# Scores of two heads as two 64-row tiles of TensorE, with the queries stacked two heads to 128 partitions

## Chip, core and metric

The kernel runs on one core of a Trainium2 chip. The metric is the device time of one execution in microseconds (us), the median over several runs.

## What is computed

The input x has 8 batches of 256 tokens with 256 features. It is normalised to xn, and two branches are computed from xn and joined:

```python
xn = _layernorm(x, axis=-1)
s  = attention_1(xn)       # 16 heads, head size 80 (64 rotary + 16), low-rank weights, causal softmax
h  = attention_2(xn)       # inside _L0_ffn_ref: RMS norm, 16 heads of size 16, causal softmax
g  = _silu(xn + h @ Wo.T + moe(rmsnorm(xn + h @ Wo.T)))   # 8 experts, top 2
out = x + s * g
```

The change touches attention_2 (called "mha" in the kernel) alone: `attn = softmax(causal(q @ k.T / 4))` for 16 heads of size 16 and 256 tokens, and `attn @ v`.

## The kernel before, in words

The work runs over eight batches b; batches 1 to 6 are a hardware loop, 0 and 7 are written out. After them come 23 expert blocks (the last 300 us), which the change doesn't touch. Each batch has four stages, and each engine runs its own list in this order; semaphores alone tie the engines together.

- **P2** (`stage_p2`, L689): TensorE turns the stacked queries and keys of attention_2 (`qs`, `ks`, one token to a partition) by eight steps u of four 128x128 transposes each. Steps with even u are queries, with odd u keys; `bank2(u)` (L356) rotates over three PSUM banks, so step u waits until bank u-3 has been copied out. A transposed bank holds four head pairs: the even head of a pair on partitions 0 to 63, the odd one on 64 to 127. The keys are kept like that (`kt2`, two heads to 128 partitions). The queries are not: `qt2` has a slot of 128 partitions for each of the 16 heads, the other half of which is zero (set once by POOL, L485), so that a matmul over all 128 rows against the pair's keys gives one head's scores. ACT copies the even heads (L1073, semaphore `t2e`) and DVE the odd heads (`odd_heads`, L1422, semaphore `t2o`). DVE also normalises the previous batch's attention_2 here (L1307).
- **T1** (`stage_t1`, L779): for every head h of attention_1, `scores1` (L769) computes its transposed scores into bank 4 + h % 2, ACT takes the exponential (L1094) and DVE masks it (`causal`, L1386). Between them stand the plain scores of attention_2 for the row maximum: `max2` (L727) computes head h into bank 2 + h % 2, and DVE takes its maximum in two instructions (`maxima`, L1399 and L1402). TensorE's order in `heads` (L757) is: scores of head h, then the maximum's scores of head h-1, then for h = 7, 11, 15 the products with the values of four heads (`values`, L744), then what `after` hangs on head h: the previous batch's transposes back (0) and output projection (3), the transposes of the next x (10), the router's transposes (11, they wait for DVE's L1496) and logits (14). DVE's order (`stage_m2`, L1388) is: causal(h), maxima(h), then what hangs on h: the residual (4), statistics (5), a copy of x (7), the scaling for the router (9, L1496), the low part of x (12). After head 15 DVE picks the top two experts (L1507 to L1522), and TensorE waits for that early in P1.
- **P1** (`stage_p1`, L638): the projections of the next batch, transposed head by head.
- **T2** (`stage_t2`, L786): for every head h of attention_2, `scores2` (L773) computes its transposed scores (two matmuls with the queries and keys, two that add the mask from bf16 tiles) into bank 4 + h % 2 for ACT's exponential. Between them stand the plain scores of attention_1 of the next batch, `max1` (L714), with DVE's maxima. ACT also rounds keys for max1 (`rounded`, L1019) after every even head from 2 to 12, DVE rounds queries (L1358).

The rule that one bank belongs to even heads and the other to odd heads holds in both stages: head h waits only for the release of head h-2 (`mx2`, `mx1`, `ex1`, `ex2`, each to the count h-1).

Of the kernel before, what the change touches and what calls it, by code (L numbers as in the profile page):

```python
# [91 lines left out]
def build(nc, x, w_cols, w_dq, w_uqr, w_dkv, w_ukv, w_out, w_o, w_ln1, w_ln2, w_r, w_experts,  # L92
          cosines, sines, ident, mask, mask_t, seen_t, upper, route_c, slots, out):
    ctx = ExitStack()
    with ctx:
# [84 lines left out]
        qt2 = sb("qt2", [P, H, S], F32R, late)  # L180
# [100 lines left out]
        t2o = sem("mha_q_odd_kept")  # L281
# [187 lines left out]
        def _(pool):  # L469
# [14 lines left out]
            nc.gpsimd.memset(ks[:, :, :, MROW2:MROW2 + 1].bitcast(F32), 1.0)  # L484
            nc.gpsimd.memset(qt2[:, :, :].bitcast(F32), 0.0).then_inc(clear, 1)  # L485
# [87 lines left out]
        def _(pe):  # L573
# [195 lines left out]
            def scores1(h, o):  # L769
                mm(o[:, P:2 * P], kt[:, h, P:S], qt[:, h, P:S], True, True)  # L770
                return mm(o[:, 2 * P:4 * P], kt[:, h, 0:P], qt[:, h, :], True, True)

            def scores2(h, o):  # L773
                mm(o[:, 0:2 * P], kt2[:, h // 2, P:S], qt2[:, h, :], True, False)
                mm(o[:, 2 * P:4 * P], kt2[:, h // 2, 0:P], qt2[:, h, :], False, False)
                mm(o[:, P:2 * P], idb[:, :], maskb[:, :], False, True)
                return mm(o[:, 2 * P:3 * P], idb[:, :], maskb[:, :], False, True)

            def stage_t1(b, after):  # L779
# [4 lines left out]
                return heads(b, scores1, st1, ex1, exm1, pv1, ov1, v1, before_h0, lambda: wait(pe, x2d, b), max2(b), after)  # L784
# [978 lines left out]
```

## Time and profile before

| | us |
|---|---|
| median of 3 runs | 976.75 |
| lowest, highest | 970.0, 980.24 |
| the profiled execution | 980.88 |
| its span, first to last instruction | 979.1 |
| TensorE busy in the span | 838.6 (86%) |
| DVE busy | 662.8 (68%) |
| ACT busy | 502.0 (51%) |
| granted TensorE clock, mean | 0.945 |

The time of an execution is 1.8 us above its span. A batch of the loop takes 78.5 us (TensorE's transposes of the row maxima start at 300.95 and again at 379.49). Busy times are shares of the whole span and mix the stages; the stages have different limits, so the rows below are taken from one batch, the one between these two times.

### The profile page before, as it was taken

How to read it: one execution, taken by the hardware profiler on the slowest of the kernel's cores; microseconds unless marked ns; L12 is line 12 of the kernel's file. 1: busy time of each engine (PE TensorE's matmuls, PEld its weight loads, DVE VectorE, ACT ScalarE, POOL GpSimd, SP SyncE). 2: the span in 40 equal slices, each digit the busy share in tenths (PEclk: the TensorE clock that was granted, in tenths of full speed). 3: DMA queues.
4: the chain of work that ended last, by engine and by line, in shares of the span. 5: the costliest groups of instructions: out<-in, count | busy, mean ns of one | idle time of the engine just before them, and what ended most of it. 6: DMA issues, size and time to landing. Idle time of an engine off the chain costs nothing.

```text
span 979.1 us, 20037 instructions
## 1 busy us (share of the span) xinstructions
PE 838.6 (86%) x6688; PEld 748.5 (76%) x6688; DVE 662.8 (68%) x2345; ACT 502.0 (51%) x1090; POOL 268.6 (27%) x286
## 2 busy tenths in 40 slices
PE   5879999999989999998998999976169999999940
PEld 3858988977887887797797797764169999999940
DVE  4877668667667766857866866833257777777726
ACT  3436465365356456355445536533046777777721
POOL 5520400320230221131041032010404454545333
PEclk9988999999999999999999999977589999999985
DMA  8000000000000000000000000030245656588434
GB/s 272 1 1 2 13 2 12 13 2 2 22 0 2 12 11 2 12 11 2 11 12 1 12 12 1 2 141 22 41 137 188 241 191 240 191 302 302 166 119 171
DMA packets 33535, 70.88 MB, mean 72 GB/s; under 512 B 10786, under 2 KB 24994, under 8 KB 30498
## 3 DMA queue, kind: packets, MB, share of 16 engines
q1 hardware_dynamic: 26866, 57.39, 16.8%
q0 software_dynamic: 5440, 12.13, 4.0%
q10 hardware_dynamic: 1152, 0.49, 0.3%
q8 instruction: 29, 0.48, 0.2%
q14 instruction: 48, 0.39, 0.2%
HBM read 57.35 MB, written 12.71 MB: 72 GB/s over the span
## 4 chain that ended last, share of the span: by engine, by line
PE 67%; DVE 14%; issue 9%; DMA 3%; SPq 3%; ACT 2%; POOL 1%; DVEq 0%; ACTq 0%; POOLq 0%
PE ps L575 55%; PE ps L668 5%; PE ps L705 3%; DVE ps L1399 2%; DVE ps L1402 2%; DVE negm L1402 1%; PE ps L601 1%; SPq L422 1%; DMA ln<-in_w_ln 1%; DVE negm L1399 1%; PE ps L902 1%; DMA yl<-expert_rows 1%; PE ps L610 1%; SPq L437 1%; DMA raw<-in_w_experts 1%
## 5 line engine op out<-in xcount | busy, mean ns | idle before, releaser
L1094 ACT ACTIVATE ex<-ps 128x384 f32<-128x384 f32 x256 | 125.6, 496 | 137.9 <-PE ps L575 126.6
L575 PE MATMUL ps<-qt,kt 128*128 128x256 f32 (+1 forms) x768 | 164.9, 325 | 9.5 <-issue 6.0
L503 POOL TENSOR_TENSOR tok<-tok,swp 128x256 f32<-128x256 f32 x128 | 97.2, 760 | 219.2 <-DVE swp L1354 218.2
L1399 DVE CUSTOM_DVE_ANT_0 ps<-ps,mask 128x128 f32<-128x128 f32 x256 | 76.4, 298 | 77.7 <-PE ps L575 45.3
L575 PEld LDWEIGHTS ps<-qt,kt 128*128 128x128 f32 x768 | 109.2, 193 | 18.6 <-issue 10.4
L1402 DVE CUSTOM_DVE_ANT_0 ps<-ps,mask 128x256 f32<-128x256 f32 x256 | 119.3, 466 | 0.0
L1233 DVE TENSOR_TENSOR wel<-raw,weh 128x768 fp32r<-128x768 f32 x92 | 88.2, 958 | 37.8 <-ACT weh L962 36.4
L575 PE MATMUL ps<-wh,xth 128*128 128x320 f32 (+2 forms) x352 | 95.7, 354 | 6.3 <-DVE wl L1233 3.7
L1350 DVE TENSOR_TENSOR tok<-ps,cos_t 128x320 f32<-128x320 f32 x128 | 62.8, 491 | 52.6 <-PE ps L575 46.8
L546 POOL DMA_INDIRECT expert_rows<-yo,slot_of x46 | 57.5, 1249 | 128.9 <-ACT yo L1195 121.9
L575 PE MATMUL ps<-xeh,weh 128*128 128x256 f32 x368 | 78.5, 295 | 11.7 <-issue 11.7
L962 ACT ACTIVATE qt<-ps 128x512 f32<-128x512 f32 (+1 forms) x96 | 57.1, 594 | 61.4 <-PE ps L668 54.7
L962 ACT ACTIVATE kt<-ps 128x512 f32<-128x512 f32 (+1 forms) x96 | 57.3, 597 | 57.4 <-PE ps L668 49.4
L962 ACT ACTIVATE weh<-raw 128x768 fp32r<-128x768 f32 x92 | 77.8, 846 | 9.9 <-DMA raw<-in_w_experts 9.7
L575 PE MATMUL ps<-wl,xth 128*128 128x320 f32 (+2 forms) x352 | 82.5, 316 | 0.0
L575 PE MATMUL ps<-wh,xtl 128*128 128x320 f32 (+2 forms) x352 | 82.4, 316 | 0.0
L668 PE MATMUL ps<-idf,tok 128*128 128x128 f32 x512 | 76.8, 272 | 0.0
L575 PE MATMUL ps<-kr,qr 128*128 128x128 f32 (+1 forms) x256 | 61.5, 325 | 17.0 <-DVE negm L1402 13.6
L575 PE MATMUL ps<-kt,qt 128*128 128x128 f32 (+1 forms) x256 | 72.0, 363 | 4.1 <-DVE negm L1402 4.1
L575 PE MATMUL ps<-xeh,wel 128*128 128x256 f32 x368 | 74.8, 285 | 0.0
L575 PE MATMUL ps<-xel,weh 128*128 128x256 f32 x368 | 74.8, 285 | 0.0
L575 PEld LDWEIGHTS ps<-xeh,weh 128*128 128x128 f32 x368 | 57.9, 195 | 15.7 <-issue 15.7
(167 smaller groups left out, 1958.4 us busy)
## 6 DMA issues: line engine op xcount, KB each, us to landing
raw<-in_w_experts SPq DMA_DIRECT2D x23, 1536.0 KB
yl<-expert_rows SPq DMA_DIRECT2D x4, 1024.0 KB, 5.4
mla_branch<-s_b SPq DMA_DIRECT2D x8, 256.0 KB, 2.1
x_normalised<-otk SPq DMA_DIRECT2D x8, 256.0 KB, 2.2
xr<-in_x SPq DMA_DIRECT2D x1, 2048.0 KB
s_tok<-mla_branch SPq DMA_DIRECT2D x1, 2048.0 KB
out<-xr SPq DMA_DIRECT2D x4, 512.0 KB, 2.9
w_cols_raw<-in_w_cols SPq DMA_DIRECT2D x1, 1792.0 KB, 15.9
```

The source lines that it names most:

```text
L422: sp.dma_start(mt_b[:, blk, :, :], rows.rearrange("(j p) f -> p j f", p=P)).then_inc(mtd[blk], 16)
L503: nc.gpsimd.tensor_tensor(t, t, swp[:, n % 2, :, :], ALU.add).then_inc(tokd, 1)
L546: nc.gpsimd.indirect_dma_start(ys[:, :], bass.IndirectOffsetOnAxis(mt_b[:, blk, j, 1:2], 0), yo[:, blk % 2, j, :], None).then_inc(ysd[blk ...
L575: return nc.tensor.matmul(o, a, m, start=start, stop=stop, skip_group_check=True, **k)
L668: t = nc.tensor.transpose(ps[2 + n % 2][:, j * P:(j + 1) * P], tok[:, n % 4, j, :], idf[:, :])
L705: i = nc.tensor.transpose(bank2(u)[:, j * P:(j + 1) * P], a[:, p0:p0 + P], idf[:, :])
L962: return nc.scalar.activation(o, a, ACT.Copy)
L1094: nc.scalar.activation(ex[:, h % (2 * G), :], ps[4 + h % 2][:, P:4 * P], ACT.Exp, scale=scale).then_inc(ex_, 1)
L1233: return nc.vector.tensor_tensor(o, a, b.bitcast(F32), ALU.subtract)
L1350: nc.vector.tensor_tensor(tok[:, n % 4, :, 0:HW], a, cos_t[:, tt:tt + 1, :].broadcast_to([P, G, HW]), ALU.mult)
L1399: nc.vector.tensor_tensor_reduce(out=o[:, 0:P], in0=o[:, 0:P], in1=mask2[:, 1, :], scale=-1.0, scalar=-2.0 * BIG, op0=ALU.add, op1=ALU.min ...
L1402: nc.vector.tensor_tensor_reduce(out=o[:, S:2 * S], in0=o[:, S:2 * S], in1=mask2[:, :, :].rearrange("p a k -> p (a k)"), scale=-1.0, scala ...
```

## The change

`qt2` becomes as wide as `kt2`: two heads to 128 partitions, no zero halves. POOL's memset of `qt2`, DVE's four `odd_heads` copies and the semaphore `t2o` go; ACT copies each transposed query bank whole. The scores are computed per pair of heads, on odd h in `max2` and on even h in `scores2`, with `tile_position=(0, 0)` for the even head and `(64, 0)` for the odd head of the pair, each into its own bank. Both banks must be free before the pair starts. The order of the pair's matmuls alternates between the tiles; the mask is added by 128-row matmuls as before.

```diff
-        qt2 = sb("qt2", [P, H, S], F32R, late)
+        qt2 = sb("qt2", [P, H // 2, S], F32R, late)
...
-            nc.gpsimd.memset(qt2[:, :, :].bitcast(F32), 0.0).then_inc(clear, 1)
...
                     if u >= 3:
 
                         wait(pe, t2e, 8 * b + u - 2)
-                        if (u - 3) % 2 == 0:
-                            wait(pe, t2o, 4 * b + (u - 3) // 2 + 1)
...
             def max2(b):
                 def head(h):
-                    if h == 0:
+                    if h % 2 == 0:
+                        return
+                    if h == 1:
                         wait(pe, t2e, 8 * b + 8)
-                        wait(pe, t2o, 4 * b + 4)
-                    if h >= 2:
+                    else:
                         wait(pe, mx2, 16 * b + h - 1)
-                    raw_scores(ps[2 + h % 2], qt2[:, h, :], kt2[:, h // 2, :]).then_inc(m2d, 1)
+                    for q0, k1, o0, first in ((0, P, 0, True), (P, S, S, False)):
+                        for e in range(2):
+                            r = slice(ST * e, ST * (e + 1))
+                            i = mm(ps[2 + e][:, o0:o0 + k1], qt2[r, h // 2, q0:q0 + P], kt2[r, h // 2, 0:k1],
+                                   first, True, tile_position=(ST * e, 0))
+                            if not first:
+                                i.then_inc(m2d, 1)
...
-            def scores2(h, o):
-                mm(o[:, 0:2 * P], kt2[:, h // 2, P:S], qt2[:, h, :], True, False)
-                mm(o[:, 2 * P:4 * P], kt2[:, h // 2, 0:P], qt2[:, h, :], False, False)
-                mm(o[:, P:2 * P], idb[:, :], maskb[:, :], False, True)
-                return mm(o[:, 2 * P:3 * P], idb[:, :], maskb[:, :], False, True)
+            def scores2(b):
+                def head(h):
+                    if h % 2:
+                        return
+                    if h >= 2:
+                        wait(pe, ex2, 16 * b + h)
+                    for k in range(1, -1, -1):
+                        for e in range(2):
+                            r = slice(ST * e, ST * (e + 1))
+                            mm(ps[4 + e][:, (1 - k) * S:(2 - k) * S], kt2[r, h // 2, k * P:(k + 1) * P],
+                               qt2[r, h // 2, :], k == 1, False, tile_position=(ST * e, 0))
+                    for e in range(2):
+                        mm(ps[4 + e][:, P:2 * P], idb[:, :], maskb[:, :], False, True)
+                        mm(ps[4 + e][:, 2 * P:3 * P], idb[:, :], maskb[:, :], False, True).then_inc(st2, 1)
+                return head
...
-                    if u % 2 == 0:
-
-                        h0 = 8 * (u // 2 % 2)
-                        copy(qt2[0:ST, h0:h0 + 8:2, t], a[0:ST, :, :]).then_inc(t2e, 1)
-                    else:
-                        copy(kt2[:, 4 * (u // 2 % 2):4 * (u // 2 % 2) + 4, t], a).then_inc(t2e, 1)
+                    h0 = 4 * (u // 2 % 2)
+                    copy((qt2, kt2)[u % 2][:, h0:h0 + 4, t], a).then_inc(t2e, 1)
...
-                wait(dve, st2, 16 * b)
-                odd_heads(b, 0)
-                odd_heads(b, 1)
-                odd_heads(b, 2)
                 normalise()
-                odd_heads(b, 3)
```

`scores1` keeps its instructions and its wait for head h-2; only its place in the code moves. The two small DMAs that write the maxima into row 48 and 112 of `qt2` (L393) write whole rows instead of every second head's.

## Rows read from the trace of the kernel before

**Rows 1.** The page: the chain that ended last, by engine, then by line.
```profile
PE 67%; DVE 14%; issue 9%; DMA 3%; SPq 3%; ACT 2%; POOL 1%; DVEq 0%; ACTq 0%; POOLq 0%
PE ps L575 55%; PE ps L668 5%; PE ps L705 3%; DVE ps L1399 2%; DVE ps L1402 2%; DVE negm L1402 1%; PE ps L601 1%; SPq L422 1%; DMA ln<-in_w_ln 1%; DVE negm L1399 1%; PE ps L902 1%; DMA yl<-expert_rows 1%; PE ps L610 1%; SPq L437 1%; DMA raw<-in_w_experts 1%
```

**Rows 2.** Windows T1, P1, T2, P2: length, PE, PEld, DVE, ACT, POOL busy; PEclk; DMA.
```profile
307.60:331.50 23.90, 22.56 (x190) 18.47 (x188) 20.04 (x103) 11.06 (x26) 0.86 (x1) 1.00 0.03 11
331.50:357.60 26.10, 26.10 (x192) 25.45 (x193) 15.56 (x39) 11.05 (x21) 11.93 (x16) 1.00 0.03 11
357.60:379.50 21.90, 18.72 (x187) 14.79 (x186) 16.50 (x92) 13.09 (x32) 3.92 (x4) 1.00 0.01 1
300.95:307.60 6.65, 6.28 (x52) 5.58 (x53) 3.78 (x8) 5.00 (x11) 0.00 (x0) 1.00 0.02 5
```

**Rows 3.** Tile qt (qt and qt2 together): copies and memset, min/median/max ns, first and last start.
```profile
L1229 DVE CAST qt<-ps x32: 686/695/696, 75.2 to 620.5; 64x512 fp32r<-64x512 f32 x32
L485 POOL MEMSET qt<- x1: 3517/3517/3517, 7.6 to 7.6; 128x4096 f32 x1
```

**Rows 4.** Timeline of P2, PE then ACT: start us, us, operation, [idle before <-releaser].
```profile
303.90 0.66 PE L705 MATMUL ps<-idf,ks 128*128 128x128 f32 x4 [0.37 <-DVE qt L1229]
...
307.14 0.49 ACT L1094 ACTIVATE ex<-ps 128x384 f32<-128x384 f32 x1
```

**Rows 5.** Timeline of T1, PE. qt,kt: scores1; kt,qt: max2; wo,otf: project; ex,v: values.
```profile
310.11 1.89 PE L575 MATMUL ps<-wo,otf 128*128 128x256 f32 x8
311.84 0.82 PE L575 MATMUL ps<-qt,kt 128*128 128x128 f32 x4
312.31 0.58 PE L575 MATMUL ps<-kt,qt 128*128 128x128 f32 x2
312.72 0.82 PE L575 MATMUL ps<-qt,kt 128*128 128x128 f32 x4
...
315.46 0.86 PE L575 MATMUL ps<-ex,v 128*32 128x256 f32 x16
316.25 0.92 PE L575 MATMUL ps<-qt,kt 128*128 128x128 f32 x4
316.82 0.58 PE L575 MATMUL ps<-kt,qt 128*128 128x128 f32 x2
```

**Rows 6.** Timeline of T1, DVE: maxima of head 3, causal of head 4.
```profile
313.03 0.30 DVE L1399 CUSTOM_DVE_ANT_0 ps<-ps,mask 128x128 f32<-128x128 f32 x1 [1.50 <-PE ps L575]
...
313.63 0.14 DVE L1402 DVE_READ_ACCUMULATOR2_ANT negm<- 128x1 f32 x1
313.63 0.42 DVE L1386 TENSOR_TENSOR ex<-ex,seen 128x256 f32<-128x256 f32 x1
313.96 0.29 DVE L1399 CUSTOM_DVE_ANT_0 ps<-ps,mask 128x128 f32<-128x128 f32 x1
```

**Rows 7.** Waits of DVE inside T1: us in total, times, longest us.
```profile
DVE ps L1399 <- PE ps L575: 3.3, 5, 1.5
```

**Rows 8.** Timeline of T2, PE: scores2, its mask, max1.
```profile
365.10 0.40 PE L575 MATMUL ps<-qt,kt 128*128 128x256 f32 x2
365.34 0.29 PE L575 MATMUL ps<-maskb,idb 128*128 128x128 bf16 x2
365.43 0.48 PE L575 MATMUL ps<-kr,qr 128*128 128x128 f32 x2
```

**Rows 9.** Timeline of T2, ACT and DVE around a joint wait.
```profile
365.66 0.49 ACT L1094 ACTIVATE ex<-ps 128x384 f32<-128x384 f32 x1 [3.04 <-PE ps L575]
366.05 0.62 ACT L962 ACTIVATE kr<-kt 128x512 fp32r<-128x512 f32 x1
366.56 0.48 ACT L1094 ACTIVATE ex<-ps 128x384 f32<-128x384 f32 x1
369.38 0.49 ACT L1094 ACTIVATE ex<-ps 128x384 f32<-128x384 f32 x1 [2.33 <-PE ps L575]
369.53 0.30 DVE L1399 CUSTOM_DVE_ANT_0 ps<-ps,mask 128x128 f32<-128x128 f32 x1 [1.42 <-PE ps L575]
```

More of the change, by code:

```diff
@@ L483, in _ @@
             nc.gpsimd.memset(tok[:, 1:4:2, :, MROW:MROW + 1], 1.0)
-            nc.gpsimd.memset(ks[:, :, :, MROW2:MROW2 + 1].bitcast(F32), 1.0)
-            nc.gpsimd.memset(qt2[:, :, :].bitcast(F32), 0.0).then_inc(clear, 1)
+            nc.gpsimd.memset(ks[:, :, :, MROW2:MROW2 + 1].bitcast(F32), 1.0).then_inc(clear, 1)
             def power(k, t):
@@ L757, in heads @@
                 for h in range(H):
-                    if h >= 2:
-                        wait(pe, ex_, 16 * b + h - 1)
-                    scores_t(h, ps[4 + h % 2]).then_inc(st, 1)
+                    scores_t(h)
                     if h > 0:
@@ L767, in heads, with scores1, head @@
                 return lambda: values(NG - 1)
-            def scores1(h, o):
-                mm(o[:, P:2 * P], kt[:, h, P:S], qt[:, h, P:S], True, True)
-                return mm(o[:, 2 * P:4 * P], kt[:, h, 0:P], qt[:, h, :], True, True)
-            def scores2(h, o):
-                mm(o[:, 0:2 * P], kt2[:, h // 2, P:S], qt2[:, h, :], True, False)
-                mm(o[:, 2 * P:4 * P], kt2[:, h // 2, 0:P], qt2[:, h, :], False, False)
-                mm(o[:, P:2 * P], idb[:, :], maskb[:, :], False, True)
-                return mm(o[:, 2 * P:3 * P], idb[:, :], maskb[:, :], False, True)
+            def scores1(b):
+                def head(h):
+                    o = ps[4 + h % 2]
+                    if h >= 2:
+                        wait(pe, ex1, 16 * b + h - 1)
+                    mm(o[:, P:2 * P], kt[:, h, P:S], qt[:, h, P:S], True, True)
+                    mm(o[:, 2 * P:4 * P], kt[:, h, 0:P], qt[:, h, :], True, True).then_inc(st1, 1)
+                return head
+            def scores2(b):
+                def head(h):
+                    if h % 2:
+                        return
+                    if h >= 2:
+                        wait(pe, ex2, 16 * b + h)
[7 more added lines that the diff above has]
+                        mm(ps[4 + e][:, 2 * P:3 * P], idb[:, :], maskb[:, :], False, True).then_inc(st2, 1)
+                return head
             def stage_t1(b, after):
@@ L783, in before_h0 @@
                     wait(pe, v1d, 2 * b + 2)
-                return heads(b, scores1, st1, ex1, exm1, pv1, ov1, v1, before_h0, lambda: wait(pe, x2d, b), max2(b), after)
+                return heads(b, scores1(b), exm1, pv1, ov1, v1, before_h0, lambda: wait(pe, x2d, b), max2(b), after)
             def stage_t2(b, max_head, after):
@@ L790, in before_h0 @@
                     wait(pe, v2d, b + 1)
-                heads(b, scores2, st2, ex2, ex2, pv2, ov2, v2, before_h0, lambda: wait(pe, sd, b + 1), max_head,
+                heads(b, scores2(b), ex2, pv2, ov2, v2, before_h0, lambda: wait(pe, sd, b + 1), max_head,
                       after)()
@@ L1420, in low2 @@
                     op0=ALU.mult, op1=ALU.subtract).then_inc(s2d, 1)
-            def odd_heads(b, i):
-                wait(dve, tr2, 8 * b + 2 * i + 1)
-                t = slice(i // 2 * P, (i // 2 + 1) * P)
-                h0 = 8 * (i % 2)
-                copy(qt2[ST:P, h0 + 1:h0 + 8:2, t],
-                     bank2(2 * i)[ST:P, :].rearrange("p (h t) -> p h t", h=4)).then_inc(t2o, 1)
             def batch(b, first, more):
                 normalise, kept = ((lambda: None),) * 2 if first else close2(b - 1)
-                wait(dve, st2, 16 * b)
-                odd_heads(b, 0)
-                odd_heads(b, 1)
-                odd_heads(b, 2)
                 normalise()
-                odd_heads(b, 3)
                 after = {4: kept}
```

5 lines of the change are left out of this document (2 added, 3 removed).

## Prediction

> **What bounds the kernel now.** First the chain that ended last [rows 1]: 67% of it is TensorE, 55% in the one matmul helper, 14% DVE, and nearly all of DVE's named lines are the row maxima (L1399, L1402). So TensorE leads, and DVE leads in places. Where, the windows of one batch tell [rows 2]. P1 (26.1 us) is TensorE without a gap, and the change doesn't touch it. T1 is 23.9 us with TensorE busy 22.6 and DVE 20.0: two engines close to full, coupled head by head. T2 is 21.9 us with 18.7, 16.5 and 13.1 (ACT): nobody is full, so what counts there is the hand-over between them. P2 is 6.65 us. The granted clock is 1.00, that is 2.4 GHz, in all four. The change takes work off TensorE and DVE in T1, T2 and P2 and pays in hand-overs, so I walk the stages with the durations of single instructions rather than with busy shares. Waits of DVE for the max scores in T1 are only 3.3 us in five places [rows 7]: that is all that faster matmuls could give back to DVE there.
>
> **Small parts.** POOL's memset ran from 7.6 to 11.1 us [rows 3] while the first weights were still on their way; POOL's next work depends on DVE's statistics of x, so it gives 0. If that cover were gone it would be at most its 3.5 us, once. DVE's 32 copies of 0.69 us [rows 3] go: 2.8 us of DVE per batch, all in P2. ACT's query copy becomes 128 partitions in place of 64; its 64-partition form takes about what the neighbouring full copies do (0.6 us either way in P2), so I add 0. The DMAs into the mask rows keep their bytes; 0.
>
> **P2: -0.5 us per batch.** Transposing step u = 3 started at 303.90 after an idle 0.37 whose releaser is DVE's copy [rows 4]. Without that copy, steps are limited by TensorE (0.44 us a step) and ACT (0.5 us a copy): ACT's eighth copy ends, and the exponential of head 0 starts, near 306.65 in place of 307.14 [rows 4], and TensorE's first scores move from 306.28 to about 305.7. Bounds 0 to -0.9; I take -0.5. DVE's normalising moves earlier too, but its user was not late.
>
> **T1: what a pair costs.** Today head h's max scores go into one bank while DVE reads the other. DVE takes 0.60 us for a maximum (313.03 to 313.63) and 0.33 for the mask of a head (313.63 to 313.96) [rows 6], 0.93 together; TensorE takes 0.47 for scores1 and 0.41 for max2, 0.88 together [rows 5]. They run side by side with a bank in hand. After the change one pair fills both banks, so TensorE may start it only when DVE has read both. That is a ping-pong:
> - end of DVE's last maximum to the pair's start: the accumulator read ends 0.14 after DVE could go on [rows 6], plus 0.05 for the semaphore (estimate);
> - the pair itself: four matmuls. If the two tiles run at the same time, it occupies TensorE as long as one head does now, 0.41 us [rows 5]. Each change of array shape costs extra: after the values (128x32 tiles) scores1 occupies 316.25 to 316.82, 0.57 in place of 0.47 [rows 5], so 0.1. The shape changes twice a pair, once inside this path. I take 0.52. No row shows two row tiles at once. Bounds: 0.3 (both tiles free of any cost, close to max1's 0.32 for one head) and 0.82 + 0.2 (no overlap);
> - to DVE's start: max2 at 312.31 + 0.41 = 312.72, DVE at 313.03 [rows 5, 6], so 0.31.
> Sum 1.02 us from DVE free to DVE's next maximum. DVE has 0.33 of masking to do meanwhile, so about 0.7 us idle per pair, where nothing else stands between.
>
> The Trainium skill says the same of the shape change: a change of tiling mode, not of tile, drains the engine (TensorEngine Tiling, Key Properties). The trace agrees with its 0.1 us. By a free change the T1 term below would be 0.7 us less per batch, T2's 0.6 less.
>
> **T1: the walk of one batch.** DVE idle before the first maximum of each pair:
> - heads 0, 1: now issued behind scores of head 2, which wait for exponential 0 (306.65 + 0.49 + 0.05); 0.47 + 0.52 + 0.31 later is 308.5; DVE has masked head 0 by 307.5: 1.0.
> - heads 2, 3: behind scores 3, the projection (1.73 [rows 5]) and scores 4: 308.2 + 0.5 + 1.73 + 0.47 + 0.52 + 0.31 = 311.7; DVE free at 310.4: 1.3.
> - heads 4, 12, 14: the bare 0.7 each: 2.1. Head 6: hidden behind DVE's statistics after head 5 (1.4 us). Head 8: 0.7 less the 0.34 of the copy of x after head 7: 0.4.
> - heads 10, 11: this pair now stands behind the router's transposes, which wait for DVE's L1496 after head 9 (near 323.0 in this walk); today max2 of head 10 stands ahead of them. 323.0 + 0.5 + 0.47 + 0.52 + 0.31 = 324.9, DVE free at 323.2: 1.7.
> Together 6.5 us in place of 3.3 [rows 7]: +3.2, or +2.8 when I walk the unchanged kernel by the same steps (which finds 3.7). DVE's work of T1 is unchanged and sets its end, since the choice of experts follows the last maximum on DVE and TensorE waits for it in P1. With P2's -0.5: **+2.5 us per batch for P2 and T1**. With the pair at 0.3 it is +0.8, at 1.02 +5.9. TensorE's saved 3.3 us (eight times 0.41) become waiting.
>
> **T2: +1.1 us per batch.** For two heads TensorE needs now 2 x (0.24 + 0.09 + 0.32) = 1.3 us [rows 8], so it isn't the limit; DVE needs 2 x 0.6 for maxima, 0.33 for rounding and mostly 0.4 of splits, 1.9 us. New: the pair waits for both exponentials. Its loop is 0.24 (two tiles at once) + 0.18 (four masks) + 0.1 (shape change inside) on TensorE, 0.23 to ACT (365.43 to 365.66 [rows 8, 9]), 0.39 exponential, 0.51 rounding of keys, 0.49 exponential [rows 9], 0.05: 2.2 us, 0.3 above DVE's 1.9. Also max1 of the odd head, which could go earlier, is queued behind the pair that waits, and DVE waits for it. Six such rounds give +1.6 to +1.8; in the two rounds with an added projection (1.4 us) the loop is as long before as after. Against this, ACT and DVE both wait around 368 to 369.5 though TensorE's scores are recorded as done (2.33 and 1.42 idle [rows 9]); part of the new waits will fall into such holes. I take off 0.5. Bounds: -1.0 (the holes swallow all, and TensorE's saved 0.24 a pair counts) and +3.4 (no overlap of tiles). What is late next in both stages is DVE's maximum.
>
> **Sum.** 8 batches x 2.5 = 20, T2 7 x 1.1 = 8 (the last T2 has no maxima; ACT alone, +0.3). 28 us. On the profiled execution's own time, 980.9 (span 979.1 and 1.8 around it), that is 1009. The median stands 4.1 us below that execution, so the forecast for the median is 976.75 + 28, some **1004 us**, +2.8%.
>
> **Rivals.**
> - A, faster: the stages follow TensorE's work, not the hand-over. Place: T1 and T2. Then per batch P2's 0.5, the 1.5 idle that DVE has behind the projection and about 1.5 us of T2's joint waits go: 3.5 us, 28 in all, 949. For it: T1 has TensorE 94% busy and it is 67% of the chain. Against: DVE is 84% busy there and its 3.3 idle can't go below zero, while the pair needs both banks. It decides when the way from DVE's last maximum to the next falls from 1.02 below 0.33 us; the semaphore and tail alone are 0.5. Chance 0.07.
> - B, the tiles don't overlap (the change does not do what it says): pair 1.02, scores2's pair 0.24 longer. T1 +5.9, T2 +2.9, 8.5 a batch, about 1045. For it: no row shows row tiles. Against: the column tiles of the values do overlap, 16 matmuls with 4 x 2 x (256 + 128) = 3072 columns in 0.79 us (315.46 to 316.25 [rows 5]), where one after the other they would take 1.28 at 2.4 GHz. The Trainium skill has row tiles starting about 4 ns apart (TensorE: Matmul & The Clock Gate, The mechanism); no row here shows that. Chance 0.08.
> - C, nearly nothing: the pair takes 0.3, a shape change is hidden by weight loads, and T2's holes swallow its new waits: T1 +0.8, T2 +0.2, 8 us, 985. Chance 0.17.
> - The clock: TensorE idles more in T1, in pieces up to 1.8 us. Today's T2 leaves it idle 3.2 of 21.9 us at clock 1.00 [rows 2]. Should it fall, the start of P1 would run at half speed, some 2 us a batch more: 1020, inside the range; counted with the forecast.
>
> **How the numbers follow.** Forecast 0.68, A 0.07, B 0.08, C 0.17. The forecast's own range: T1 +1.7 to +3.1, T2 +0.3 to +2.2, so 16 to 42 us: 993 to 1019. Range for 8 in 10: 979 (most of C) to 1030. About 1% can be told from no change in a measurement of this kernel, 967 to 986.5. Faster: 0.07. Same: 0.13 (much of C). Slower: 0.80.
>
> **What would show it.** Right: in T1 DVE's wait for TensorE rises from 3.3 to some 6 us in seven places, each even head's maximum late, the one of head 10 most; TensorE's busy time in T1 falls by about 3 us; P1 keeps 26.1 us; P2's first exponential comes 0.5 us sooner; in T2 exponentials come in twos 2.2 us apart. A batch takes about 82 us. Wrong: a batch below 78.5 us, or odd heads' maxima waiting (then the tiles don't overlap), or a clock below 1.00 in P1, which would make another term of the sum.

## The result, and the profile after

| us | before | after |
|---|---|---|
| median of 4 runs | 975.14 | 1016.52 |
| lowest, highest | 970.0, 980.24 | 1014.64, 1017.0 |
| the profiled execution | 980.88 | 1016.31 |
| its span | 979.1 | 1014.5 |
| granted clock, mean | 0.945 | 0.930 |

The ratio is 1.0421, with an interval of 1.0385 to 1.0456: 41 us slower by the medians, 35.4 us by the two profiled spans. The forecast was 1004 (979 to 1030). Ratios leave out one execution, the profiled one of e2 below, which took 1036.33 us where the fastest of the same kernel took 1018.11.

The stages of one loop batch of the kernel after, in the order P2, T1, P1, T2 (columns as in [rows 2]; the cuts are the starts of the maxima's transposes, of the first scores1, of the first projection and of the first scores2):

```profile
316.38:321.16 4.78, 4.78 (x42) 4.50 (x43) 1.13 (x4) 3.57 (x8) 0.00 (x0) 1.00 0.03 7
321.16:349.19 28.03, 24.62 (x199) 17.42 (x197) 20.17 (x102) 12.24 (x28) 0.86 (x1) 1.00 0.03 10
349.19:375.48 26.29, 26.29 (x192) 25.48 (x193) 15.54 (x39) 11.06 (x20) 11.95 (x16) 1.00 0.03 11
375.48:399.02 23.54, 18.94 (x184) 14.10 (x184) 16.61 (x92) 14.12 (x32) 3.93 (x4) 0.93 0.01 1
```

[Rows 2] cut the batch a little otherwise: they count TensorE's first scores1 (from 306.28) with P2. By the cuts used here the kernel before has P2 5.33, T1 25.21 (TensorE busy 23.87), P1 26.12, T2 21.88, together 78.54. All lengths from here on are by these cuts.

| one loop batch | before | after | difference | forecast |
|---|---|---|---|---|
| P2 | 5.33 | 4.78 | -0.55 | -0.5 |
| T1 | 25.21 | 28.03 | +2.82 | +3.0 |
| P1 | 26.12 | 26.29 | +0.17 | 0 |
| T2 | 21.88 | 23.54 | +1.66 | +1.1 |
| batch | 78.54 | 82.64 | +4.1 | +3.6 |

Over the whole span: first batch +5.55, the six loop batches +23.45, P2 and T1 of the last batch +3.31, the last T2 and everything behind it +3.1; together 35.4. The six T2 of the loop give 8.7 of the 23.45, and 6.6 of that is what four of them take above the two that kept a granted clock of 1.00.

**T1.** The waits of DVE between 323 and 349.2 (columns as in [rows 7], which it answers to):

```profile
DVE ps L1411 <- PE ps L573: 5.9, 6, 1.7
```

and four of the six in DVE's timeline, the first maxima of heads 0, 2, 4 and 10:

```profile
324.30 0.30 DVE L1411 CUSTOM_DVE_ANT_0 ps<-ps,mask 128x128 f32<-128x128 f32 x1 [1.33 <-PE ps L573]
...
327.96 0.30 DVE L1411 CUSTOM_DVE_ANT_0 ps<-ps,mask 128x128 f32<-128x128 f32 x1 [1.71 <-PE ps L573]
...
330.32 0.30 DVE L1411 CUSTOM_DVE_ANT_0 ps<-ps,mask 128x128 f32<-128x128 f32 x1 [0.41 <-PE ps L573]
...
340.72 0.30 DVE L1411 CUSTOM_DVE_ANT_0 ps<-ps,mask 128x128 f32<-128x128 f32 x1 [1.61 <-PE ps L573]
```

All six stand before an even head (0, 2, 4, 10, 12, 14: 1.33, 1.71, 0.41, 1.61, 0.41, 0.42), none before an odd one. TensorE's timeline there (answers to [rows 5]):

```profile
326.57 0.82 PE L573 MATMUL ps<-qt,kt 128*128 128x128 f32 x4
327.32 0.50 PE L573 MATMUL ps<-kt,qt 64*128 64x128 f32 x4
327.75 1.58 PE L573 MATMUL ps<-qt,kt 128*128 128x128 f32 x8
329.68 0.50 PE L573 MATMUL ps<-kt,qt 64*128 64x128 f32 x4 [0.36 <-DVE negm L1414]
```

The pair's four tile matmuls occupy 327.32 to 327.75, 0.43 us, as long as one head's two did before (0.41). But scores1 ahead of them now occupies 0.75 (326.57 to 327.32) instead of 0.47. The second pair waits for DVE's accumulator read (0.36): that is the hand-over of both banks.

**T2.** TensorE, around the third and fourth pair and a projection (answers to [rows 8]):

```profile
379.50 0.50 PE L573 MATMUL ps<-qt,kt 64*128 64x256 f32 x4 [0.93 <-ACT ex L1106]
379.94 0.40 PE L573 MATMUL ps<-maskb,idb 128*128 128x128 bf16 x4
380.14 0.47 PE L573 MATMUL ps<-kr,qr 128*128 128x128 f32 x2
381.68 0.77 PE L573 MATMUL ps<-kr,qr 128*128 128x128 f32 x2 [1.06 <-DVE negm L1414]
382.25 0.63 PE L573 MATMUL ps<-wh,xth 128*128 128x256 f32 x2
382.67 0.63 PE L573 MATMUL ps<-wl,xth 128*128 128x256 f32 x2
```

The pair waits for ACT's exponential (0.93) and takes 0.44 for its four tile matmuls; two heads took 2 x 0.24 in [rows 8]. After the 1.06 us hole two matmuls of 256 columns are 0.42 us apart (382.25 to 382.67); at the full clock they are 0.23 to 0.24 apart (shown with the last run below). So the engine runs at the lower level, 1.2 GHz, from some point in the hole to about 384.9. Four of the loop's six T2 have such a stretch (granted clock 0.86 once, 0.93 three times, lengths 24.37, 23.62, 23.54 and 23.53 us); the other two keep 1.00 and take 22.12 and 22.13. In the kernel before, the six T2 take 21.40 to 21.88, all at a clock of 1.00, though each has a longer hole at the same place (363.42 is TensorE's next matmul after it):

```profile
363.42 0.47 PE L575 MATMUL ps<-kr,qr 128*128 128x128 f32 x2 [1.48 <-DVE negm L1402]
363.73 0.40 PE L575 MATMUL ps<-wh,xth 128*128 128x256 f32 x2
363.96 0.39 PE L575 MATMUL ps<-wl,xth 128*128 128x256 f32 x2
```

So such a hole doesn't lower the clock by itself.

ACT's exponentials come in twos (answers to [rows 9]; in the one hole of 3.91 us the half-speed projection stands in front of the scores):

```profile
377.98 0.49 ACT L1106 ACTIVATE ex<-ps 128x384 f32<-128x384 f32 x1
...
380.26 0.49 ACT L1106 ACTIVATE ex<-ps 128x384 f32<-128x384 f32 x1 [0.72 <-PE ps L573]
...
385.63 0.49 ACT L1106 ACTIVATE ex<-ps 128x384 f32<-128x384 f32 x1 [3.91 <-PE ps L573]
...
387.91 0.49 ACT L1106 ACTIVATE ex<-ps 128x384 f32<-128x384 f32 x1 [0.81 <-PE ps L573]
```

380.26 less 377.98 and 387.91 less 385.63 are both 2.28 us. The joint waits of [rows 9] are gone: after TensorE has finished its scores, nobody waits.

### The profile page after: what moved, and what is told of

Read it like the earlier page. It is cut to its first block, busy times and chain, and to the rows that moved or that the text cites. A ratio compares the mean times of both kernels' runs of the same rounds, so it can differ in the third digit from the quotient of the medians.

```text
span 1014.5 us, 19947 instructions
## 1 busy us (share of the span) xinstructions
PE 847.4 (84%) x6688; PEld 725.4 (72%) x6688; DVE 644.1 (63%) x2313; ACT 506.7 (50%) x1090; POOL 264.8 (26%) x285
## 4 chain that ended last, share of the span: by engine, by line
PE 66%; DVE 15%; issue 8%; ACT 3%; DMA 3%; SPq 2%; POOL 1%; DVEq 0%; ACTq 0%; POOLq 0%
PE ps L573 54%; PE ps L666 5%; DVE ps L1411 3%; PE ps L701 3%; DVE ps L1414 2%; ACT ex L1106 2%; PE ps L599 1%; DVE negm L1414 1%; DVE negm L1411 1%; SPq L421 1%; PE ps L918 1%; PE ps L608 1%; DMA yl<-expert_rows 1%; DMA w_ukv_raw<-in_w_ukv 1%; SPq L436 1%
## 5 line engine op out<-in xcount | busy, mean ns | idle before, releaser
L1106 ACT ACTIVATE ex<-ps 128x384 f32<-128x384 f32 x256 | 123.4, 489 | 164.6 <-PE ps L573 162.8
L573 PE MATMUL ps<-qt,kt 128*128 128x128 f32 (+2 forms) x768 | 139.5, 342 | 27.4 <-ACT ex L1106 23.4
L573 PEld LDWEIGHTS ps<-qt,kt 128*128 128x128 f32 (+1 forms) x768 | 90.7, 193 | 49.3 <-ACT ex L1106 32.7
L1398 DVE TENSOR_TENSOR ex<-ex,seen 128x256 f32<-128x256 f32 x128 | 53.7, 419 | 28.3 <-ACT ex L1106 28.3
L1193 ACT ACTIVATE sg<-ps 128x256 f32<-128x256 f32 x92 | 35.8, 389 | 67.2 <-PE ps L573 67.2
```

What stands on the lines that cost most here:

```text
L573: return nc.tensor.matmul(o, a, m, start=start, stop=stop, skip_group_check=True, **k)
L1106: nc.scalar.activation(ex[:, h % (2 * G), :], ps[4 + h % 2][:, P:4 * P], ACT.Exp, scale=scale).then_inc(ex_, 1)
L1193: nc.scalar.activation(sg[:, n % 2, :], ps[n % 3][:, 0:BS], ACT.Silu).then_inc(sgd, 1)
L1398: nc.vector.tensor_tensor(a, a, seen[:, 0:1, :].broadcast_to([P, 2, P]), ALU.min).then_inc(exm1, 1)
```

## The experiments

H is the theory that the loss is the hand-over of both banks at once, X that it is the changes of array shape. The later ones are R (row tiles lower the clock), S (POOL's indirect DMAs make T2's joint waits) and K (the hole in T2 lowers the clock). Each run has its own measurements of the kernel before beside it, which its ratio stands against. Medians are of all executions. Lengths are those of loop batches in the profiled execution, "@" is the granted clock of that T2.

| run | median us | ratio (interval) | T1 | T2 |
|---|---|---|---|---|
| e2_t1_single | 1028.74 | 1.0514 (1.0456, 1.0572) | 28.73 | 23.54@.93 to 28.65@.70 |
| e3_t2_single | 1016.12 | 1.0425 (1.0355, 1.0495) | 28.02 | 22.47@1.00, 23.88@.93, 29.35@.71 |
| e4_t1_pair_full | 998.41 | 1.0242 (1.0221, 1.0263) | 27.84 | 20.67@1.00, 22.23@.92 |
| e5_pair_early | 1011.06 | 1.0365 (1.0342, 1.0388) | 26.61 | 23.63@.93, 24.15 to 24.24@.86 |
| e9_full_pair_early | 1005.44 | 1.0248 (1.0215, 1.0281) | 26.62 | 21.24, 21.81@1.00, 24.69@.93, 26.3@.87 |
| e7_fill_t2 | 1058.44 | 1.0801 (1.0781, 1.0821) | 28.03 | 28.85 to 29.60@.88 |
| e8_early_fill | 1045.01 | 1.0659 (1.0638, 1.0681) | 26.61 | 28.77 to 29.90@.88 |
| e10_t2_pair_full | 1017.18 | 1.0372 (1.0349, 1.0395) | 25.20 | 26.04@.93, 28.19@.88 |
| e12_before_scatter_t1 | 976.88 | 0.9979 (0.9955, 1.0003) | 25.47 | 20.68@1.00, 22.27@.92 |
| e11_after_scatter_t1 | 1020.60 | 1.0450 (1.0372, 1.0528) | 28.14 | 22.11@1.00, 23.63@.93, 24.71@.86 |
| e14_changed_fill_hole | 1020.88 | 1.0392 (1.0347, 1.0437) | 28.39 | 22.12@1.00, 23.27@.93, 24.61@.86 |
| e15_before_fill_hole | 976.89 | 0.9964 (0.9949, 0.9979) | 25.74 | 20.67 to 20.73@1.00 |

e7, e8, e14 and e15 add matmuls whose results nothing reads; all other runs do the same computation in another order.

### Is T1's loss the hand-over or the shape change?

**e4_t1_pair_full**: the kernel before, 128-row matmuls, no tiles; only max2 is issued in pairs, with the changed kernel's wait.

```diff
-                    if h == 0:
+                    if h % 2 == 0:
+                        return
+                    if h == 1:
                         wait(pe, t2e, 8 * b + 8)
                         wait(pe, t2o, 4 * b + 4)
-                    if h >= 2:
+                    else:
                         wait(pe, mx2, 16 * b + h - 1)
-                    raw_scores(ps[2 + h % 2], qt2[:, h, :], kt2[:, h // 2, :]).then_inc(m2d, 1)
+                    for g in (h - 1, h):
+                        raw_scores(ps[2 + g % 2], qt2[:, g, :], kt2[:, g // 2, :]).then_inc(m2d, 1)
```

> The kernel before, with its 128-row matmuls and zero halves, but max2 issues heads h-1 and h together at odd h, waiting for both banks (T1 only); no shape changes are added. H: a pair takes 0.82 us and DVE idles about 1.1 us where it idles 0.7 to 0.4 in the changed kernel: T1 +4 to +4.8 us a batch, 975 + 32 to 38 = 1007 to 1013. X: no shape change, so no loss, about 975.

Measured: 998.41 us. Its windows of one T1, one T2 at the full clock and one below it:

```profile
312.34:340.18 27.84, 24.24 (x198) 19.02 (x196) 21.61 (x105) 12.27 (x28) 0.86 (x1) 1.00 0.03 10
366.30:386.97 20.67, 18.55 (x187) 14.69 (x185) 16.49 (x92) 13.22 (x32) 3.99 (x4) 1.00 0.01 1
446.21:468.44 22.23, 20.11 (x187) 16.19 (x185) 16.50 (x92) 13.22 (x32) 4.00 (x4) 0.92 0.01 1
```

and DVE's first three waits for the maximum's scores in that T1:

```profile
315.37 0.30 DVE L1402 CUSTOM_DVE_ANT_0 ps<-ps,mask 128x128 f32<-128x128 f32 x1 [1.21 <-PE ps L575]
...
318.86 0.30 DVE L1402 CUSTOM_DVE_ANT_0 ps<-ps,mask 128x128 f32<-128x128 f32 x1 [1.55 <-PE ps L575]
...
321.23 0.30 DVE L1402 CUSTOM_DVE_ANT_0 ps<-ps,mask 128x128 f32<-128x128 f32 x1 [0.42 <-PE ps L575]
```

Without one tile T1 loses 2.63 of the 2.82 us, with the waits at the same heads (the others 1.41, 0.42, 0.45). So the hand-over of both banks is enough for a loss of this size, and X falls for T1: with no shape change it expected none. The whole came out lower than H's number: it had put 4 to 4.8 on T1. H took a pair at its whole 0.82 us, but DVE needs only the even head's two matmuls to go on: with the pair started at 320.58 it goes on at 321.23, 0.65 us later, as in the changed kernel (0.64). And T2 became shorter in three of six batches (20.67 against 21.88), which neither theory had; in the other three the clock fell to 0.92 (22.25), in stages whose code is that of the kernel before.

**e2_t1_single**: the changed kernel, with max2 for each head alone on its tile and the old wait for head h-2. It has the tiles but not the hand-over.

```diff
-                    if h % 2 == 0:
-                        return
...
-                        for e in range(2):
-                            r = slice(ST * e, ST * (e + 1))
+                    e = h % 2
+                    r = slice(ST * e, ST * (e + 1))
```

> The changed kernel, but max2 issues each head's tile by itself into its own bank, with the old wait for head h-2 (T1 only). Theory H (the hand-over of two banks at once costs T1 its 2.8 us a batch): DVE's seven waits shrink to what they were, T1 falls from 28.0 to about 25.2 us, 1016.5 - 8 x 2.8 = about 994. Theory X (the change between 128-row and 64-row matmuls, 0.28 us on each side as the changed trace seems to show, is the cost): twice as many changes, TensorE needs about 0.47 + 0.28 + 0.21 + 0.28 = 1.24 us a head against DVE's 0.93, T1 about 5 us longer than before the change, above 1030.

Measured: 1028.74 us. One T1 in its windows:

```profile
330.42:359.15 28.73, 28.54 (x199) 19.27 (x197) 20.56 (x102) 12.34 (x28) 0.86 (x1) 1.00 0.03 9
```

and TensorE's timeline in it:

```profile
338.23 0.92 PE L573 MATMUL ps<-qt,kt 128*128 128x128 f32 x4
339.09 0.49 PE L573 MATMUL ps<-kt,qt 64*128 64x128 f32 x2
339.51 0.92 PE L573 MATMUL ps<-qt,kt 128*128 128x128 f32 x4
```

Two things follow. One head's two tile matmuls take 0.42 (339.09 to 339.51), what the pair's four take, so in a pair the two tiles do run side by side. And scores1 between tiles takes 0.86, 0.39 more than before (0.47), with TensorE busy 28.54 of 28.73: changing the shape for every head makes TensorE the bound. So for this form the cost is the one X names, at 3.5 us of T1 instead of the 5 it expected. The shape change and the hand-over can't both be avoided with tiles: pairs halve the first and bring the second. The 1028.74 us are not T1's alone, which is only 0.7 longer than the changed kernel's: the six T2, whose code is that of the changed kernel, all ran below the full clock in this profile (23.5 to 28.7 us).

**e5_pair_early** issues the pair one head earlier in TensorE's list, on even h, ahead of scores1 of the odd head and of what hangs on it; **e9_full_pair_early** does the same with e4's 128-row pairs.

```diff
-                    if h % 2 == 0:
+                    if h % 2:
                         return
-                    if h == 1:
+                    if h == 0:
                         wait(pe, t2e, 8 * b + 8)
                     else:
-                        wait(pe, mx2, 16 * b + h - 1)
+                        wait(pe, mx2, 16 * b + h)
```

> The changed kernel, but the pair (h, h+1) of max2 is issued in the place of the even head, one head earlier: ahead of the projection for heads 2 and 3, ahead of the router's transposes for heads 10 and 11. H with the queue order as part of it: the 1.33, 1.71 and 1.61 us waits of DVE at heads 0, 2 and 10 fall to the bare 0.4, T1 -3 us a batch, about 993. X: the number of shape changes is the same, so the time stays at 1016 within 3 us. A third outcome: TensorE now stands in the wait for DVE with scores1 queued behind it, ACT's exponential comes late, and the gain is less than half.

> The kernel before (128-row matmuls, no tiles) with max2 in pairs, the pair one head earlier. With the pair at the later place T1 was 27.8 us, and its waits fell at the same heads as in the changed kernel. Theory H with the queue order: moving the pair takes off 1.3 us as it did with tiles (28.0 to 26.6), T1 about 26.5, time about 998 - 10 = 988. Rival: the gain of 1.4 needed the short pair (0.43 us), and with 0.82 on TensorE, which is then the limit of T1, less than half of it comes: 994 or more.

Measured: T1 26.61 and 26.62, 1.4 and 1.2 us less than with the pair late. About half of the loss was thus the place in the queue: behind the projection and the router's transposes. The waits left before maxima in e5 are 0.68, 0.42, 0.24, 0.16 and 0.62; two of 1.33 and 0.84 now stand before DVE's masking, which waits for ACT, since scores1 comes behind the pair. That is the third outcome of the expectation: less than half of the 3 us came. The time of e5 fell by 5.5 us, not by 8 x 1.4 = 11, since its T2 ran below the full clock in all six loop batches. For e9 the T1 came as expected and the time didn't: its T2 rose to 26.3 in three batches, at a clock of 0.87, in two of them with a joint wait (ACT 3.64, DVE 2.72 us) such as e7 shows below.

### Where T2's loss comes from

**e3_t2_single**: the changed kernel, scores2 for each head alone on its tile, waiting for head h-2.

```diff
-                    if h % 2:
-                        return
                     if h >= 2:
-                        wait(pe, ex2, 16 * b + h)
+                        wait(pe, ex2, 16 * b + h - 1)
...
-                        for e in range(2):
-                            r = slice(ST * e, ST * (e + 1))
+                    e = h % 2
+                    r = slice(ST * e, ST * (e + 1))
```

> The changed kernel, but scores2 issues each head by itself with the old wait for head h-2 (T2 only). H: T2 loses its 1.7 us a batch, 1016.5 - 13 = about 1003. X: TensorE needs about 0.24 + 0.28 + 0.09 + 0.32 + 0.28 = 1.2 us a head against 0.95 on DVE, T2 gets 2 to 4 us longer, 1032 or more. Theory K (half of T2's loss is the clock, which fell to 1.2 GHz for some 2.5 us in the changed T2): with fewer holes in TensorE's work the clock is 1.00 again, -1.2 us a batch at least, about 1006.

Measured: 1016.12, between what H and K expected and what X did, and 10 us or more from each. One T2 at the full clock:

```profile
380.15:402.62 22.47, 21.34 (x184) 14.98 (x184) 16.52 (x92) 13.75 (x32) 3.91 (x4) 1.00 0.01 1
```

It takes 22.47 with TensorE busy 21.34, against 22.12 in pairs. As in T1, the shape changes take what the hand-over gave. Its runs spread from 1009.61 to 1024.13, and in the longest, which is the profiled one, one T2 had a granted clock of 0.71 and took 29.35, while four took 22.47: the clock decides more than the form.

**e7_fill_t2** and **e8_early_fill**: ten bf16 matmuls into bank 4 ahead of every scores2 pair, to keep TensorE working while it waits; e8 has e5's early pair as well.

```diff
                     if h >= 2:
+                        wait(pe, ex2, 16 * b + h - 1)
+                        for _ in range(10):
+                            mm(ps[4][:, 0:P], idb[:, :], idb[:, :], True, True)
                         wait(pe, ex2, 16 * b + h)
```

> The changed kernel with work added: ten bf16 128x128 matmuls per pair in T2, into an unread part of bank 4, issued when exponential h-2 is done and before the wait for exponential h-1, so that TensorE isn't idle there. K (T2's holes let the clock fall to 1.2 GHz in most batches, and that is most of T2's loss): clock 1.00 in every T2 of the loop, T2 22.1 to 22.4 us in place of 23.5, time 1016.5 - 6 x 1.4 - a bit for the last batch = about 1006. Rival R (the clock falls because 64-row matmuls are little work to it, whatever the holes): clock stays at 0.93 and the time at 1016 or above.

> Both mendings of the changed kernel: max2's pair one head earlier and the added matmuls in T2. K: T1 26.6, T2 22.2 at clock 1.00 in place of 24.2 at 0.86, a batch 79.9 us, 1011 - 12 = about 998. It is still above the kernel before by the hand-over left in T1 (1.4 us a batch) and P1, T2 0.2 and 0.3. R: no better than 1011.

Measured: 1058.44 and 1045.01, T2 near 29 us at a clock of 0.88. Both expectations failed. In e7's timeline of all engines between 400 and 404:

```profile
400.29 0.96 POOL L516 DMA_INDIRECT slots<-meta,posu  x1 [0.30 <-issue]
...
400.33 0.70 PE L573 MATMUL ps<-kr,qr 128*128 128x128 f32 x4
...
401.55 0.96 POOL L516 DMA_INDIRECT slots<-meta,posu  x1 [0.30 <-issue]
403.54 0.49 ACT L1109 ACTIVATE ex<-ps 128x384 f32<-128x384 f32 x1 [4.36 <-remote]
403.73 0.30 DVE L1414 CUSTOM_DVE_ANT_0 ps<-ps,mask 128x128 f32<-128x128 f32 x1 [3.45 <-remote]
```

TensorE's scores are recorded as done by 401.1, and neither ACT nor DVE starts before 403.5. This looks like the joint wait of [rows 9], but longer: ACT sat idle for 4.36 us and DVE for 3.45, in [rows 9] for 2.33 and 1.42. POOL issues its four indirect DMAs just there (397.68, 399.02, 400.29, 401.55).

**e10_t2_pair_full**: the kernel before, scores2 in pairs of 128-row matmuls.

```diff
-                    if h >= 2:
-                        wait(pe, ex_, 16 * b + h - 1)
-                    scores_t(h, ps[4 + h % 2]).then_inc(st, 1)
+                    if ex_ is ex2:
+                        if h % 2 == 0:
+                            if h >= 2:
+                                wait(pe, ex_, 16 * b + h)
+                            for g in (h, h + 1):
+                                scores_t(g, ps[4 + g % 2]).then_inc(st, 1)
...
```

> The kernel before with scores2 in pairs (T2 only), both with 128-row matmuls, after a wait for both banks. H by the walk of the prediction: T2 +0.2 (at full clock, as between 21.9 and the changed kernel's 22.1) to +1.6 us a batch: 976 to 987. K: the hand-over alone lets the clock fall as well, then T2 is 23 to 23.5 us in most batches, about 988. R: without 64-row matmuls the clock stays at 1.00.

Measured: 1017.18. Two T2 in its windows:

```profile
371.31:399.50 28.19, 22.03 (x186) 17.45 (x185) 16.70 (x92) 14.24 (x32) 4.11 (x4) 0.88 0.01 1
456.26:482.30 26.04, 20.42 (x186) 16.00 (x185) 16.70 (x92) 14.24 (x32) 3.91 (x4) 0.93 0.01 1
```

The clock falls here with no row tile in the kernel, as it does in e4, so row tiles aren't needed for it and R falls. Waits of 2.54 us (ACT) and 2.30 (DVE) stand again beside POOL's DMAs. So these stages can't price the hand-over of T2 by themselves: it is mixed with both.

The first batch can. Its T2 has no indirect DMA, no joint wait and a clock of 1.00 in the kernel before, here and in the changed kernel; the windows in this order:

```profile
125.54:144.65 19.11, 18.52 (x182) 14.66 (x179) 14.82 (x78) 13.12 (x31) 0.00 (x0) 1.00 0.01 1
125.59:147.67 22.08, 18.45 (x182) 14.46 (x180) 15.14 (x78) 14.16 (x31) 0.00 (x0) 1.00 0.01 1
129.37:150.20 20.83, 17.12 (x179) 12.45 (x178) 15.24 (x78) 14.02 (x31) 0.00 (x0) 1.00 0.01 2
```

In e4, whose T1 alone is in pairs, this stage takes 19.05, so T1's form doesn't touch it. The hand-over with 128-row matmuls costs 2.97 us there, and the tiles give 1.25 of it back: a pair's scores start 2.50 us after the last ones without tiles (127.28 to 129.78) and 2.28 with them (131.12 to 133.40).

**e12_before_scatter_t1** and **e11_after_scatter_t1**: POOL's four indirect DMAs, which write the slots of a batch, wait for the T1 of the next batch, in the kernel before and in the changed one.

```diff
-            with pool.Fori(1, last) as b:
+            power2(0)
+            rope_sums(2)
+            with pool.Fori(2, last) as b:
                 power2(b - 1)
+                scatter_slots(b - 2)
                 rope_sums(b + 1)
-                scatter_slots(b - 1)
             power2(last - 1)
+            scatter_slots(last - 2)
             scatter_slots(last - 1)
```

> The kernel before, with POOL's four small indirect DMAs of a batch (L518) moved from the middle of T2 to T1 of the next batch. Theory S (the joint waits of ACT and DVE in T2, 1.4 + 1.4 us in the kernel before, 2 to 4 us in the runs with paired 128-row scores2 or with added matmuls, fall together with these DMAs and come from them): T2 falls from 21.9 to about 20.6 us, as in the one run where the waits were missing (T1 in pairs), unless T1 now gets them: 975 - 10 = 965, or 975 where they move into T1. Rival: the waits are of another origin, T2 stays at 21.9.

> The changed kernel, with the same move of POOL's indirect DMAs to T1. Its T2 shows no joint waits, so S expects little in T2 (22.1 to 23.5 us, by the clock), and at worst a wait of 1 to 3 us in T1: 1016, up to 1030. If T2 gets shorter here too, part of what I gave to the hand-over in T2 was this.

Two T2 of e12 (POOL has nothing in them now):

```profile
358.86:379.54 20.68, 18.53 (x187) 14.69 (x185) 16.51 (x92) 13.20 (x32) 0.00 (x0) 1.00 0.00 0
436.39:458.66 22.27, 20.12 (x186) 16.22 (x184) 16.50 (x92) 13.31 (x32) 0.00 (x0) 0.92 0.00 0
```

The joint waits are gone, and T2 at the full clock is 20.68 instead of 21.88: taking the DMAs away is enough to be rid of the waits. They are not enough to bring them: e4 and the changed kernel issue the same four DMAs in T2 (e4 from 375.20, the changed kernel from 384.79) and show no joint wait. In four of e12's six loop batches the clock fell and took 1.6 back, and T1 grew by 0.26, so the whole is 0.9979, no change that can be told. TensorE's timeline around the hole of one of the four:

```profile
442.20 0.47 PE L578 MATMUL ps<-kr,qr 128*128 128x128 f32 x2 [1.48 <-DVE negm L1405]
...
442.74 0.57 PE L578 MATMUL ps<-wl,xth 128*128 128x256 f32 x2
443.11 0.64 PE L578 MATMUL ps<-wh,xtl 128*128 128x256 f32 x2
```

The hole is the one that the kernel before has at 363.42, where the clock stayed. The changed kernel had no joint waits to lose; it came out at 1020.6, its T2 as before.

This gives the comparison that e10 could not: at the full clock and with no joint waits, T2 takes 20.68 in the old form and 22.12 in the new, +1.44.

### Does filling the hole keep the clock?

**e14_changed_fill_hole** is e11 with 14 bf16 matmuls into bank 6 behind head 4 of T2; **e15_before_fill_hole** is e12 with 18 of them behind scores2 of head 5.

```diff
+                    after[4] = lambda: [mm(ps[6][:, 0:P], idb[:, :], idb[:, :], True, True) for _ in range(14)]
```

```diff
...
-                return mm(o[:, 2 * P:3 * P], idb[:, :], maskb[:, :], False, True)
+                i = mm(o[:, 2 * P:3 * P], idb[:, :], maskb[:, :], False, True)
+                if h == 5 and fill5[0]:
+                    i.then_inc(st2, 1)
+                    for _ in range(18):
+                        mm(ps[6][:, 0:P], idb[:, :], idb[:, :], True, True)
+                    return None
+                return i
```

> The changed kernel with POOL's indirect DMAs in T1 (its T2 without this addition: 22.3, 24.7, 23.6, 23.6, 22.1 us in five batches, short at clock 1.00, long below it) and with 14 bf16 matmuls into the unused bank 6 in T2 behind head 4, where TensorE stands idle 1.06 us for DVE before the clock falls. K (the hole lets the clock fall): every T2 of the loop at clock 1.00 and 22.1 to 22.3 us, about 1.2 us less a batch, 1020 - 8 = about 1012. R (64-row matmuls lower it, not the hole): T2 stays at 23.5 on average, 1020.

> The kernel before with POOL's indirect DMAs in T1 (its T2 then: 20.7 us at clock 1.00 in two batches, 22.3 with the clock fallen in four) and 18 bf16 matmuls into bank 6 behind scores2 of head 5, where TensorE stands idle 1.45 us. K: 20.7 to 20.8 us and clock 1.00 in all batches of the loop, 977 - 6 to 7 = about 970, below both kernels. R: no 64-row matmul is here, so R has nothing to say; if the clock still falls, the hole isn't its cause: 977.

e14 missed K's number and met R's (1020, T2 at 23.5 on average), though e10 shows that the clock falls without row tiles too. Its TensorE timeline shows why it can't decide between them:

```profile
382.02 0.76 PE L576 MATMUL ps<-qt,kt 64*128 64x256 f32 x4 [0.93 <-ACT ex L1110]
```

The same four matmuls take 0.50 at the full clock: it had already fallen, behind an earlier hole of 0.93 us, before the added work began at 383.65. In e15 it held in all six T2 of the loop. One T2 in its windows, then TensorE's timeline:

```profile
357.45:378.18 20.73, 19.58 (x205) 15.72 (x203) 16.51 (x92) 13.20 (x32) 0.00 (x0) 1.00 0.00 0
```

```profile
361.62 1.17 PE L578 MATMUL ps<-idb 128*128 128x128 bf16 x18
363.26 0.47 PE L578 MATMUL ps<-kr,qr 128*128 128x128 f32 x2 [0.47 <-DVE negm L1416]
363.56 0.40 PE L578 MATMUL ps<-wh,xth 128*128 128x256 f32 x2
363.80 0.40 PE L578 MATMUL ps<-wl,xth 128*128 128x256 f32 x2
```

Here the matmuls of a projection are 0.24 apart (363.56 to 363.80). All six loop T2 take 20.67 to 20.73; in e12, where the hole before that projection was 1.48 us, four of six took 22.3. That fits K, but it is one profiled execution on each side, and it doesn't show K: the kernel before kept 1.00 in six of six with the hole open (and with the joint wait behind it). Nor do the clocks of whole executions single e15 out: 0.940 to 0.949 in its nine, 0.943 to 0.949 in the kernel before beside it. T1 grew to 25.74 (+0.53 against before, not explained), which took back a part. At 0.9964 (0.9949 to 0.9979) e15 is 3.6 us under the kernel before measured beside it, which is little.

## Why the prediction was right or wrong

**Right: the side, and T1.** The forecast walked T1 by the hand-over. It said waits of some 6 us in seven places; there are 5.9 in six. By pair the walk had 1.0, 1.3, 0.7, 0.4 (head 8), 1.7 (head 10), 0.7, 0.7; measured 1.33, 1.71, 0.41, none, 1.61, 0.41, 0.42. The bare ping-pong costs 0.41, not 0.7: from the pair's start to DVE's maximum 0.64 us pass (329.68 to 330.32), where the walk had 0.52 + 0.31, since the pair itself takes 0.43 and the change of shape is paid ahead of it. The two pairs at the front are 0.3 to 0.4 longer. The errors cancel: P2 and T1 together came to +2.27 against +2.5. e4 shows that the bank hand-over alone brings such a loss, and e5 and e9 show the share of the queue's order in it.

**Right: the tiles overlap.** Rival B falls (0.43 for four matmuls, 0.42 for two), rivals A and C too: DVE's waits did not shrink. P2's -0.55 came as argued. Two sums of the prediction are a little off (the pair of heads 10 and 11 comes to 324.8, the upper end of the forecast's own range to 40 us), and neither changes a verdict.

**Mis-sized: the shape change.** The step "shape change 0.1" was read from scores1 behind the values' column tiles [rows 5]. Measured for these row tiles: scores1 ahead of a tile takes 0.28 more, and by itself between two of them 0.39 more (e2). The same comes out of busy times: T1 of the changed kernel has 24.62 us of TensorE and e4's, with twice the work in its max scores, 24.24. The 8 x 0.41 = 3.3 us that tiling saves are all gone, and 0.4 more, which makes some 0.46 a pair (an estimate from these two busy times). That is why "TensorE's busy time in T1 falls by about 3 us" failed: it rose by 0.75. In pairs it hardly shows in T1's length (2.82 against e4's 2.63): the bare way from the pair's start to DVE's maximum is 0.64 with it and 0.65 in e4 without. The Trainium skill says that a change of mode, not of tile, drains the engine, and promises up to twice the speed for dimensions of at most 64 (TensorEngine Tiling, Key Properties and Theoretical Speedup). The trace agrees with both: scores1 takes longer next to a tile (0.75 and 0.86 for 0.47), and four tile matmuls occupy 0.43 us where two of one tile occupy 0.42. At one pair per change, T1's busy time shows that the change costs as much as the second tile gives.

**The step that failed inside a forecast that held: T2 at an unchanged clock.** "Today's T2 leaves it idle 3.2 of 21.9 us at clock 1.00" was taken to mean that it would stay so, and the clock item looked for a fall only in T1 and P1, where the clock is 1.00 in the rows after. It fell in T2, in four of the loop's six, and 23.53 or more against 22.12 makes 1.4 to 2.25 us in each, 6.6 in all. Without it the T2 term would have been +0.24 (22.12 against 21.88), less than the forecast's 1.1; that the measured T2 lies near the forecast is luck. The smaller number is again two that cancel: the new form at +1.44 (the walk had +1.6 to +1.8, and its period of 2.2 is the measured 2.28), and the old kernel's joint waits, worth 1.2 (21.88 against e12's 20.68), all gone; the forecast took off 0.5. Of the new form the first batch tells the parts: the hand-over with 128-row pairs +2.97, the tiles with their shape change -1.25, together +1.72.

**The ends of the kernel.** The first batch lost 5.55 (forecast 3.6). Its T1 has no work of a previous batch between the heads, and went from 19.46 to 23.52; e4 lost 3.8 there, so this too is the hand-over. The last T2 and what follows lost 3.1 (forecast 0.3): from the first scores2 to the first transposes of the experts' rows it is 57.06 before and 61.96 after, a loss of 4.9, of which the expert blocks give back 1.8, which isn't explained. In that T2 the pairs stand 2.4 to 2.8 us apart (scores2 at 694.75, 697.16, 699.58 and 702.39, the last two at the lower clock: 0.80 for what takes 0.50). Together these are 4.8 of the 7.4 us by which the spans' 35.4 exceed the forecast's 28. The rest is 1.85 in the six loop batches (23.45 against 21.6) and 0.8 in P2 and T1 of the last. P1's +0.17 is a shape change too, which the forecast put at 0: the first scores2 starts 0.53 us after P1's last transposes (374.95 to 375.48), 0.36 before (357.25 to 357.61), and P1 is 26.29 in e2, e3 and e5, whose scores2 has tiles, and 26.11 or 26.12 in e4, e9 and e10, whose scores2 has none. By the medians the difference is 41: the profiled execution of the kernel before stood 5.7 above its median of 975.14, the one after 0.2 below its own.

**Still open.** Which idle, of what length and after what, lowers the clock: holes of about 1 us went before it in the changed kernel and of 1.48 in e12, yet both kernels also have T2s with the same holes at 1.00, and the kernel before kept 1.00 in all six with the hole of 1.48 and, in five of them, a joint wait (DVE idle for 1.32 to 1.42) behind it. So the clock's part of the loss is measured, and its cause is open. And why ACT and DVE wait for scores that are recorded as done while POOL issues indirect DMAs: e12 shows that the waits need the DMAs, e4 that something else must come with them.

## What to carry to other kernels

A pair of operations that fills both banks of a double buffer turns it into a single one: count the way from the last reader to the next result (here 0.4 us bare, 1.3 to 1.7 where other work stands in front) against what the pair saves, and put the pair as early in the queue as its operands allow. Two row tiles do run at once, but entering and leaving their shape cost about 0.4 us here, as much as the second tile gave in T1. That they pay where many tiled matmuls follow each other is likely from that, but no run here tried it. Before a change that makes TensorE wait more in a stage where it is not the limit, look for matmul-bound work behind the new holes: what the clock takes from it can exceed the wait itself (here 1.4 to 2.25 us in a stage that was 0.24 longer without it).

## What the hardware showed that was not expected

- Row tiles: four 64-row matmuls in 0.43 us, two of one tile alone in 0.42; scores1 between tiles 0.86 in place of 0.47.
- The clock fell to 1.2 GHz in the middle of T2 for over 3 us (half-speed matmuls from 381.68 to 384.87) with no hole longer than 1.1 us before it in that T2, and in the kernel before stayed at 1.00 through six T2 with a hole of 1.48.
- Joint waits for scores that were recorded as done: DVE idle for 1.42 us (before), 2.30 (e10) and 3.45 (e7), ACT for 2.33, 2.54 and 4.36, beside POOL's indirect DMAs, and absent when these were moved (e12). In e4 and the changed kernel the DMAs stood in T2 without such a wait.
